# Marks written back into the correlation's PSUM bank, and ScalarE's even-spectrum copies put ahead of one normalisation

## The reference

```python
x = x + xattn(layernorm(x), ctx, ctx)   # autocorrelation attention, 8 heads
x = x + ffn(layernorm(x))               # 16 experts (2 per token) + one shared FFN

# xattn, for each sequence and each of the 512 channels, over the 64 positions:
corr = ifft(fft(q) * conj(fft(k))).real        # 64 lags
w, idx = top_k(corr, 8);  w = softmax(w)
out[pos] = sum_i w[i] * v[min(idx[i] + pos, 63)]
```

## Time and profile before

| | |
|---|---|
| three timed runs, median | 509.97 us |
| span of the profiled execution, first to last instruction | 507.2 us |
| pipeline over the pairs | about the first 180 us of it |
| TensorE busy, whole span | 476.8 us (94%) |
| VectorE busy | 312.2 us (62%) |
| ScalarE busy | 222.7 us (44%) |
| GpSimd busy | 227.3 us (45%) |

### The profile page before, as it was taken

The page is one execution under the profiler, slowest core; times in us unless marked ns, Lnnn a source line. Parts: engine busy times, 40 slices in busy tenths (PEclk is TensorE's granted clock), DMA queues, the critical chain, the costliest instruction groups (busy, mean ns, idle before and its releaser), DMA issues.

```text
span 507.2 us, 8574 instructions
## 1 busy us (share of the span) xinstructions
PE 476.8 (94%) x2097; PEld 328.1 (65%) x2098; DVE 312.2 (62%) x972; ACT 222.7 (44%) x425; POOL 227.3 (45%) x384
## 2 busy tenths in 40 slices
PE   4789999999999999898899999999999999999997
PEld 2556556656655655356576667766667678888885
DVE  3799899999999863884133333333333566747643
ACT  4778888888888835200122222122221435022120
POOL 2356676676667544044333333333333026466520
PEclk9899999999999999999999999999999999999999
DMA  4416533424253031801435555455554314555622
GB/s 157 163 43 237 173 110 127 145 63 146 68 180 114 36 103 43 331 0 43 124 113 157 165 165 151 150 158 161 165 153 151 131 63 126 159 174 165 207 62 83
DMA packets 24923, 66.76 MB, mean 132 GB/s; under 512 B 3456, under 2 KB 3456, under 8 KB 23488
## 3 DMA queue, kind: packets, MB, share of 16 engines
q1 hardware_dynamic: 18576, 45.74, 25.0%
q0 software_dynamic: 6320, 20.71, 15.6%
HBM read 45.73 MB, written 20.71 MB: 131 GB/s over the span
## 4 chain that ended last, share of the span: by engine, by line
PE 62%; DVE 15%; POOL 8%; issue 8%; ACT 5%; DMA 1%; SPq 0%; DVEq 0%; POOLq 0%; ACTq 0%
PE bank L457 19%; PE bank L655 17%; PE bank L670 8%; PE bank L643 4%; DVE top_v L923 4%; POOL arena L1198 4%; PE bank L469 4%; POOL arena L1201 4%; PE bank L558 2%; DVE arena L928 2%; PE bank L567 2%; DVE stats L886 2%; DVE resid L911 2%; ACT arena L772 2%; ACT arena L771 2%
## 5 line engine op out<-in xcount | busy, mean ns | idle before, releaser
L655 PEld LDWEIGHTS bank<-wgu_sb,x2T 128*128 128x128 f32 x376 | 67.6, 189 | 41.0 <-issue 33.6
L655 PE MATMUL bank<-wgu_sb,x2T 128*128 x376 | 92.0, 388 | 2.1 <-ACT x2T L814 0.6
L814 ACT COPY x2T<-bank 128x512 f32<-128x512 f32 x47 | 27.5, 585 | 142.6 <-PE bank L643 142.6
L1251 POOL DMA_INDIRECT xg_sb<-x_rows,gidx x47 | 45.9, 976 | 98.0 <-PE bank L643 93.6
L1083 DVE COPY actT_both<-bank 128x128 f32<-128x128 f32 x47 | 13.7, 291 | 73.3 <-PE bank L664 73.3
L670 PE MATMUL bank<-arena,actT_both 128*128 x94 | 47.9, 593 | 0.0
L457 PE MATMUL bank<-act_lo 128*128 128x512 f32 x96 | 41.2, 538 | 6.7 <-DVE act_lo L965 6.7
L457 PE MATMUL bank<-tokens_hi,shgu_hi 128*128 128x512 f32 x92 | 36.2, 394 | 0.0
L457 PE MATMUL bank<-tokens_hi,shgu_lo 128*128 128x512 f32 x92 | 35.8, 389 | 0.0
L457 PE MATMUL bank<-tokens_lo,shgu_hi 128*128 128x512 f32 x92 | 35.8, 389 | 0.0
L457 PEld LDWEIGHTS bank<-act_lo 128*128 128x128 f32 x96 | 18.7, 197 | 22.8 <-issue 20.8
(11 more groups left out here) (153 smaller groups left out, 1077.7 us busy)
## 6 DMA issues: line engine op xcount, KB each, us to landing
y_rows<-x2T SPq DMA_DIRECT2D x47, 256.0 KB, 3.1
wgu_sb<-w_gu SPq DMA_DIRECT2D x8, 1024.0 KB, 5.3
resid<-x SPq DMA_DIRECT2D x16, 256.0 KB, 2.8
arena<-ctx SPq DMA_DIRECT2D x16, 256.0 KB, 3.3
x_rows<-arena SPq DMA_DIRECT2D x16, 256.0 KB, 2.1
result<-resid SPq DMA_DIRECT2D x16, 256.0 KB
arena<-w_down SPq DMA_DIRECT2D x1, 3072.0 KB, 13.0
shgu_sb<-sh_gu SPq DMA_DIRECT2D x1, 2048.0 KB, 8.0
```

The source lines that it names most:

```text
L655: last = mm(ps_gu[b][:, 0:2 * INTER], xgT[b][:, c * P:(c + 1) * P], wgu_sb[:, bass.ds(at + c * 2 * INTER, 2 * INTER)], start=c == 0, stop= ...
L814: copy(xgT[b], ps_xgT[:, :]).then_inc(xgT_ready, 1)
L1251: nc.gpsimd.indirect_dma_start(xg[b], None, x2_rows[:, :], bass.IndirectOffsetOnAxis(ap=gidx[b][:, 0:1], axis=0)).then_inc(gathered[b], 16)
```

## The change

The marks are replaced in place: L932 writes back into `ps_corr` and no longer into `lagw`, and L946 reads them there. VectorE therefore waits for its own L928 (`centered`) before it marks, its wait for the transposes of the pair before (`lagwT_psum`) moves to L946, and TensorE may overwrite `ps_corr` with the next pair only once L946 of the pair before has read it (`masked` in place of `lags_marked`). ScalarE's `even_context` moves in front of the normalisation of pair n-2, in every iteration but 0, where it was earlier already.

```diff
                 if live(n, 0):
                     p, _ = pair(h, b, 0)
                     pe.wait_ge(products_ready, p + 1)
-                    wait(pe, lags_marked, p)
+                    wait(pe, masked, p)
...
+                if n != 0:
+                    even_context(h, b, n)
                 if live(n, -2):
                     p, pb = pair(h, b, -2)
                     wait(act, x2T_psum, p - 1)
                     wait(act, x2_stored[pb], 16 * half(h, b, -2))
                     normalise(1, x2n[pb], tile_of(resid, p), p, x2n_ready)
-                if n != 0:
-                    even_context(h, b, n)
...
-                    wait(dve, lagwT_psum, p)
+                    dve.wait_ge(centered, p + 1)
                     apart(dve, dve_passed)
                     for s in range(SEGS):
-                        last = nc.vector.match_replace(segs(lagw)[:, s], tops[:, s], lags[:, s], TAKEN)
+                        last = nc.vector.match_replace(lags[:, s], tops[:, s], lags[:, s], TAKEN)
                     last.then_inc(lags_marked, 1)
...
                     dve.wait_ge(lags_marked, p + 1)
-                    stt(lagw, lagw, TAKEN, expz, ALU.is_equal, ALU.mult).then_inc(masked, 1)
+                    wait(dve, lagwT_psum, p)
+                    stt(lagw, ps_corr[:, :], TAKEN, expz, ALU.is_equal, ALU.mult).then_inc(masked, 1)
```

## The result

The changed kernel takes 545.2 us (median of 4 runs, 543.83 to 545.54) against 509.84 us of the kernel before, run beside it on the same chip: a ratio of 1.069, with a 95% interval of 1.066 to 1.071. It is slower by 35 us. 533.4 us was forecast, with a range of 524 to 546 us. The profiled execution spans 543.7 us against 507.2 us, 36.5 us more. Lines from 947 on have moved by one: L947 is the old L946, L954 the old L953, L1199 and L1202 the old L1198 and L1201.

What follows compares the result with a forecast made beforehand. The ring from residual addition L911 to the next, 11.07 us, was taken as the bound; 13 x 1.76 = 22.9 us, plus 0.83, less 0.30, gave 23.4 us on 509.97: 533.4 us, range 524 to 546 us.

Steps and rivals of the forecast that it cites:

- The copies wait for L938: ScalarE's even copies start no sooner when moved ahead, since L938 of the same iteration holds them; L730 follows 0.08 us later.
- The new ring: L911, L938, copies, normalisation, transposes, output matmuls, L911: 12.83 us against 11.07, 1.76 us more in each of 13 steps.
- the first piece: In each step, L911 to the end of L938: 6.69 us before, plus 0.12 for the new wait, 6.81 us.
- TensorE's order as the link: L541 waits for the late normalisation; L466, L467 and L469 queue behind it, then L911: normalisation end to L911 3.33 us.
- Marks in PSUM at no extra price: Value loads and replaces in VectorE's marking: 0 us extra taken, bounds +0.72 and -0.48 us a step; L946 takes 0.68 us.
- The clock: Rival, chance 0.11: TensorE's wait lowers its clock, costing 1.5 us in every second step, 10 us in all: 543 us.
- the 2.2 us gap: TensorE's idle time before L541 in every step, from 105.77 until the normalisation ends at 107.96.
- The start: First two iterations: second correlation waits for L946, 0.83 us later, less 0.30 us saved in iteration 1: 0.53 us.
- the marking wait: VectorE's new wait for `centered` before marking: starts 0.04 us after L928 ends, 0.12 us later in each step.
- The old ring: Rival, chance 0.06: the path by L953, L1201 and L469 stays the longer one, saving 0.30 us per iteration: 506.6 us.
- the early copies: Rival, chance 0.06: L938 does not hold the copies, which start behind L772; 0.81 us a step more, 521.0 us.
- the 0.30 us at L953: Saving per iteration up to the odd product: L946 shorter by 0.42 us, less 0.12 us for the later marking.

Runs made afterwards that it cites:

- the third buffer: Changed kernel with a third buffer for the even context spectrum, so ScalarE's copies wait for the even products of the pair before: 521.76 us, ratio 1.023.
- The transposes behind L467: Changed kernel with TensorE's four transposes L541 issued after L466 and L467, ahead of L469, in the 13 steps: 522.34 us, ratio 1.022.
- part two alone: Kernel before with only ScalarE's even copies moved ahead of the normalisation, marks still in SBUF: 542.6 us, ratio 1.065.
- part one: The marks kept in PSUM; run alone as the changed kernel with ScalarE's order put back: 510.43 us, ratio to the kernel before 0.9995.
- the swapped order: Changed kernel with transposes L541 behind L467, plus VectorE's wide subtraction put ahead of its small one: 517.73 us, ratio 1.015.

## Why the prediction was right, and where its size was off

The measured 545.2 us lies 0.8 us inside the end of the range, and that is partly luck. The range reached so far up for a price of marking in PSUM that came out at nothing and for a rival that was given 0.11. What filled it were that rival, 8.4 us, and a start that was priced too low, with 1.1 us of a longer first load in it.

**The copies wait for L938: right.** Idle 1.09 us before L730, released by L938; with the wait taken away by the third buffer, 1.06 us a step go.

**The new ring: right, term by term.** 12.95 us against 12.83 us. L730 to L732 takes 1.77 us (1.78 expected), the end of the normalisation (126.99) to the addition 3.33 us (3.33). The difference is the first piece: L911 to the end of L938 is 6.92 us and not 6.81. VectorE starts marking 0.15 us after L928 ends (121.26 to 121.41), not 0.04: it has the wait and the separating increment there, while the row that I took the 0.04 from has the wait alone. Between L911 and L886 of the kernel before, where both stand too, it is also 0.15 us (99.15 to 99.30). The wait cost 0.23 us a step, not 0.12.

**TensorE's order as the link: right.** The transposes behind L467 gave back 23 us, the falls of the clock among them; the steps themselves went from 12.95 to 11.98 us.

**Marks in PSUM at no extra price: right.** From load to load 0.21 us in the first (121.41 to 121.62), 0.20 in the rest, and the bounds of +0.72 and -0.48 us a step can be dropped. L947 took 0.68 us in all 16 pairs:

```profile
L947 DVE SCALAR_TENSOR_TENSOR arena<-bank,arena x16: 675/679/682, 20.2 to 219.2; 128x512 f32<-128x512 f32 x16
```

**The clock: a rival that came true beside the forecast.** I gave it 0.11 and 543 us, at 1.5 us in every second step; it was 1.40 us in six of 13 steps. "Every second" had no row behind it; it came out so here, and in part two alone seven of 13 steps paid. What spaces the falls stays open. It isn't another way for the kernel to go but a consequence of the same ring: the 2.2 us gap that the sum itself produced. To hold against it that the gap is shorter than that of the start was the mistake: with a gap of 2.56 us in each step, and of 2.36 us in part two alone, the clock fell in some steps, and with 1.49 us in none. The Trainium skill, "TensorE: Matmul & The Clock Gate", section "HAM oscillation — how this bites in real kernels", has the pattern, in an example with longer gaps, after each of which the clock falls; the prediction carried that "each" over to shorter ones. The trace agrees with the pattern and not with the count: 1.00 and 0.52 alternate, so about every second step pays.

**The start: the mechanism right, the size off.** The term was 0.83 - 0.30 = 0.53 us, and 3.82 were measured: 1.10 are the load, 1.16 the wait and the later marks, against 0.83, and 1.56 the longer half clock. The half clock behind the first gap was in the rows, and the longer gap there was given no price.

These terms make the difference: in spans 530.6 us was forecast and 543.7 measured, 13.1 us more. The clock in the steps is 8.4 of it, the start 3.3, the steps at full clock, where the marking wait was too small, 1.2, and 0.2 lie behind the pipeline.

**The old ring and the early copies: wrong, as the chances said.** For the old ring the worth of part one was put at 506.6 us; alone it ran at 510.4, because L896 then waits for the copies and the start is later. I had counted the 0.30 us at L953 and not followed VectorE's own list to its next wait.

## What to carry to other kernels

Moving work ahead in an engine's list gains nothing if the moved piece is held by a semaphore that comes no sooner; what stood in its place was using that wait, and loses it. Follow the displaced piece to its consumer and then along the consumer's queue: here three output matmuls stood behind four transposes that had nothing to do with them. And where a new ring leaves TensorE with a gap in every step, price the lower clock together with the ring, not as a case of its own.

## What the runs showed of the hardware

A VectorE operation with two SBUF inputs, started while GpSimd is in one of its own, ends only behind GpSimd's. The small subtraction (64 elements in each partition) took 0.96 us in place of 0.23 and ended 0.08 us behind it, in the swapped order 0.36 us, again 0.08 us behind. The wide L946 (512 elements) of the kernel before ended at 106.29, 0.54 us behind GpSimd's odd product, which ends at 105.75:

```profile
104.46 1.29 POOL L1198 TENSOR_TENSOR arena<-arena 128x512 f32<-128x512 f32 x1 [1.06 <-ACT arena L772]
```

So it looks as if VectorE stood still and did the whole work afterwards. L946 took 1.10 us beside L1198, and 0.68 to 0.69 us in the two pairs, the first and the last, where no long GpSimd operation ran beside it. With one input in PSUM the same engine ran undisturbed: 0.69 us for the wide subtraction in the swapped order, and 0.68 us for L947 of the changed kernel, which starts at 124.34 us beside L1199 (123.36 to 124.64). That is why reading the marks from PSUM made it short; in part two alone, with the marks in SBUF, it stayed at 1.10 us. The Trainium skill, "GPSIMD Engine Reference", section "8. Key points", says that GpSimd shares its SBUF interfaces with VectorE and that they contend when VectorE's instruction has two SBUF inputs; the trace agrees.

That VectorE writes PSUM in place at the pace at which it wrote SBUF, 0.20 us from one value load to the next, no row of the kernel before had shown.
